# A four-layer attention and expert kernel: the first phase in another order, and layer 1's expert rows spread by token and choice

## The chip, the cores and the metric

The kernel runs on one core of a Trainium2 chip. The metric is the device time in microseconds of one execution. A core has TensorE (PE, its matrix engine, with PEld as its weight loads), VectorE (DVE), ScalarE (ACT), GpSimd (POOL) and SyncE (SP, which here only issues DMAs), each with its own instruction stream; they meet at semaphores.

## The reference

The input is x of 16 sequences x 128 tokens x 256 features, with a context of the same shape. Four layers each add an attention and a feed-forward part to x:

```
x = x + xattn0(layernorm(x), ctx)          # 16 heads, alibi bias and masks
x = x + ffn0(layernorm(x))                 # shared network + 8 experts on some rows
x = x + xattn1(layernorm(x), ctx)          # per token, among its 16 heads; no weights
x = x + moe1(layernorm(x))                 # 8 experts, 2 per token, hidden 512
x = x + xattn2(layernorm(x), ctx)
x = x + lora_int4(layernorm(x))
x = x + xattn3(layernorm(x), ctx)          # two attentions, three norms
x = x + moe3(layernorm(x))                 # 8 experts, 2 per token, hidden 1024
```

In moe1 a softmax over the router's 8 logits picks two experts for a token; the softmax of the two probabilities weighs their outputs: `out = sum_k weight_k * (silu(x @ gate_e) * (x @ up_e)) @ down_e`.

## The kernel before

The 2048 tokens are 16 tiles of 128, in four groups of four tiles. x stays on chip. The program has five stages.

**First phase** (31 to about 476 us). One group after another goes through layer 0 (keys and values of its context `kv`, query, attention in 8 units of two passes, output product `xo`, norm, shared network `up`/`down`, router logits `lg`). Layer 1's attention of the group before it runs beside that, on VectorE alone: it is cut into small *pieces* (`layer1_pieces`, L1761), and `some(n)` puts the next n pieces between VectorE's operations for layer 0, `until(x)` all of them up to mark x. The constants `L1_FRONT, L1_STEP = 10, 4` say how many pieces stand ahead of the first unit and behind each unit's row maxima (L1598). When the layer-1 rows of the previous group are normalised (`out_rows`), TensorE turns them (`xT3`), takes the router's logits (`lg1`), VectorE ranks the experts and finds each row's slot (`lists`, L1997), and POOL scatters the rows to the table `expert_rows_in` in DRAM with 8 indirect DMAs (`scatter`, L2484). TensorE's order in a group is: kv, xT0, q, attention, xo, xT3, lg1, xT1, shared network (with the rank product `rk` in it), lg. PSUM banks are given out by a planner in the order of the products, `k1` for group 0 and `k1f` for groups 1 to 3, which are one loop.

**Last rows** (to about 588). Layer 0's router and routed experts for the first rows, and beside them layer 1's pieces of group 3, then its list, the plan of which expert's weights each of the 39 tiles of expert rows takes (`plan_tiles`), and the last scatter.

**Experts of layer 1** (620 to 866). 39 tiles of 128 slots, in pairs (u = 0, 1). SP loads a tile's rows (L597), its expert's up and gate weights (L588, 1024 KB) and down weights (L592, 512 KB), and stores the 128 x 256 result to `expert_rows_out` (L623). ACT copies the result from PSUM (L1349).

**Phase 3** (870 to about 1278). Layers 2 and 3 by groups. For each group POOL gathers two rows of `expert_rows_out` for each token with 8 indirect DMAs (`gather`, L2493), and DVE adds them to x with their weights (`combine`, L2127 and `combine_second`, L2197, 8 `scalar_tensor_tensor` of 256 columns). At group 0 this stands before anything else; at the others it stands within the group before. Layer 3's list and scatter go to a second table, whose rows are 260 wide: 256 features, token, first expert and the weights.

**Experts of layer 3** (1278 to 1715). As those of layer 1, with more weights; here VectorE works out each slot's weight and token from the 4 extra columns (`keep_info` L2098, `slot_weights` L2080), ACT scales by the weight (L1353), and POOL adds the rows to the output with one accumulating indirect DMA per tile (L2634). SP loads the rows of a tile (L599) only when keep_info has copied the last ones' columns.

## Time and profile before

| | us |
|---|---|
| median of 3 runs | 1716.42 (1716.3 to 1718.08) |
| profiled execution | 1716.88 |
| its span | 1715.1 |
| PE busy | 1327.7 (77%) |
| PEld busy | 1078.8 (63%) |
| DVE busy | 832.6 (49%) |
| ACT busy | 433.3 (25%) |
| POOL busy | 287.6 (17%) |

The span is from the first to the last instruction of the profile; busy times are sums over the span, and the share of a stage can be far from that of the whole. The profile also names, for idle time of an engine, what ended it, and TensorE's granted clock of a stretch (PEclk, 1.00 is 2.4 GHz).

### The profile page before, as it was taken

The page shows a single profiled execution, that of the slowest core. Times are in us where ns is not written, and L with a number is a line of the kernel's source. Part 1 is how long each engine was busy: PE and PEld are TensorE (multiplying, and loading weights), DVE is VectorE, ACT ScalarE, POOL GpSimd, SP SyncE. Part 2 cuts the span into 40 slices and gives each one's busy share as a digit, 9 for nine tenths or more (in the row PEclk, how much of TensorE's full clock was granted, in tenths as well). Part 3 has the DMA queues.
Part 4 walks back from the last instruction along what each step waited for, and adds up shares of the span by engine and source line. Part 5 has one row for each costly group of instructions (what it writes and reads, how often), then busy time and mean ns, then how long its engine had stood idle before and what let it go on. Part 6 is the DMA issues. An engine that isn't in the chain of part 4 may idle for free. (4 is left out here: it accounts for less than half of the span.)

```text
span 1715.1 us, 26091 instructions
## 1 busy us (share of the span) xinstructions
PE 1327.7 (77%) x8177; PEld 1078.8 (63%) x8189; DVE 832.6 (49%) x2298; ACT 433.3 (25%) x1098; POOL 287.6 (17%) x306
## 2 busy tenths in 40 slices
PE   5877587685636248998988786877439999999997
PEld 3554444453423147888875565655329999999996
DVE  2258868778778731221233848485632222222222
ACT  2635245244112001111132232322101111111111
POOL 2010030020100020000023435351421111111111
PEclk9786686588777579999988898888759999999999
DMA  9992010010192258888820011100047888888884
GB/s 343 346 289 61 1 62 0 0 61 0 39 310 95 98 203 290 289 296 297 293 67 25 17 33 38 37 26 13 25 180 278 318 315 314 313 317 313 313 315 165
DMA packets 116307, 291.38 MB, mean 170 GB/s; under 512 B 8192, under 2 KB 90528, under 8 KB 101024
## 3 DMA queue, kind: packets, MB, share of 16 engines
q1 hardware_dynamic: 106032, 273.00, 45.5%
q0 software_dynamic: 10224, 17.77, 4.1%
q8 instruction: 24, 0.39, 0.1%
q14 instruction: 27, 0.22, 0.0%
HBM read 218.84 MB, written 71.90 MB: 170 GB/s over the span
## 5 line engine op out<-in xcount | busy, mean ns | idle before, releaser
L725 PE MATMUL bank<-norm_cols,work 128*128 128x128 f32 x3744 | 461.8, 277 | 20.8 <-DMA work<-in_moe 19.6
L725 PEld LDWEIGHTS bank<-norm_cols,work 128*128 128x128 f32 x3744 | 449.0, 193 | 38.8 <-issue 21.5
L1536 DVE TENSOR_TENSOR extra<-bank,span 128x256 f32<-128x256 f32 x234 | 99.2, 425 | 465.1 <-ACT span L1343 465.1
L725 PE MATMUL bank<-work,extra 128*128 128x256 f32 x936 | 240.0, 380 | 0.0
L1343 ACT ACTIVATE span<-bank 128x256 f32<-128x256 f32 x234 | 89.9, 384 | 541.9 <-PE bank L725 523.4
L725 PEld LDWEIGHTS bank<-work,extra 128*128 128x128 f32 x936 | 160.4, 191 | 12.5
L2634 POOL DMA_INDIRECT out_x<-att_rows,slot_token x39 | 60.7, 1556 | 378.0 <-ACT att_rows L1353 313.6
L2455 POOL TENSOR_TENSOR rstd<-var_eps,neg_half 128x4 f32<-128x4 f32 x17 | 17.3, 1018 | 501.6 <-DVE var_eps L1548 501.6
L725 PE MATMUL bank<-weights,norm_cols 128*128 128x512 f32 (+1 forms) x192 | 89.2, 614 | 12.2 <-ACT norm_cols L1374 5.5
L725 PE MATMUL bank<-work 128*128 128x256 f32 (+4 forms) x260 | 70.7, 418 | 28.0 <-ACT work L1374 12.7
L1280 ACT ACTIVATE work<-bank,row_max 128x128 f32<-128x128 f32 x256 | 69.8, 392 | 41.2 <-DVE row_max L1598 41.1
L824 PE MATMUL bank<-ident,work 128*128 128x128 f32 x256 | 53.5, 368 | 31.8 <-DVE att_rows L1536 24.7
L725 PEld LDWEIGHTS bank<-work 128*128 128x128 f32 (+1 forms) x260 | 45.6, 217 | 48.0 <-issue 20.0
L1598 DVE TENSOR_REDUCE row_max<-bank 128x4 f32<-128x512 f32 x64 | 41.1, 684 | 63.6 <-PE bank L725 63.6
L725 PE MATMUL bank<-norm_cols,weights 128*128 128x256 f32 (+1 forms) x160 | 59.2, 526 | 14.6 <-ACT norm_cols L1374 11.4
L824 PEld LDWEIGHTS bank<-ident,work 128*128 128x128 f32 x256 | 39.7, 187 | 48.7 <-DVE att_rows L1536 27.0
L725 PEld LDWEIGHTS bank<-weights,norm_cols 128*128 128x128 f32 x192 | 40.9, 226 | 46.3 <-issue 28.6
L966 PE MATMUL bank<-ident,att_cols 128*128 128x128 f32 x156 | 30.4, 277 | 46.3 <-DMA att_cols<-expert_rows_in 46.3
L2462 POOL TENSOR_TENSOR rstd<-var_eps,neg_half 128x2 f32<-128x2 f32 x48 | 35.5, 739 | 176.4 <-DVE var_eps L1548 175.9
L725 PEld LDWEIGHTS bank<-norm_cols,weights 128*128 128x128 f32 x160 | 36.2, 237 | 31.6 <-ACT norm_cols L1374 16.5
L966 PEld LDWEIGHTS bank<-ident,att_cols 128*128 128x128 f32 x156 | 21.9, 142 | 54.0 <-DMA att_cols<-expert_rows_in 46.5
L732 PE MATMUL bank<-ident,norm_rows_layer 128*128 128x128 f32 x32 | 7.9, 428 | 54.3 <-DVE norm_rows_layer L1554 54.3
(330 smaller groups left out, 1965.6 us busy)
## 6 DMA issues: line engine op xcount, KB each, us to landing
work<-in_moe SPq DMA_DIRECT2D x78, 1024.0 KB, 7.5
work<-in_moe SPq DMA_DIRECT2D x39, 2048.0 KB, 7.8
work<-in_moe SPq DMA_DIRECT2D x39, 512.0 KB, 6.1
expert_rows_in<-zero SPq DMA_DIRECT2D x3, 5590.0 KB, 47.1
expert_rows_in<-zero SPq DMA_DIRECT2D x3, 5504.0 KB, 36.0
expert_rows_out<-zero SPq DMA_DIRECT2D x3, 5504.0 KB, 33.7
att_cols<-expert_rows_in SPq DMA_DIRECT2D x39, 130.0 KB, 2.0
att_cols<-expert_rows_in SPq DMA_DIRECT2D x39, 128.0 KB, 3.3
```

Source lines behind the costliest of these rows:

```text
L725: return pe.matmul(o, l, r, start=a, stop=z)
L732: m = pe.transpose(ps[:, t * P:(t + 1) * P], rows[:, t, c * P:(c + 1) * P], ident[:, :])
L824: last = pe.transpose(ps[:, h * P:(h + 1) * P], SC[:, w, 4 * x + h, :], ident[:, :])
L966: last = pe.transpose(ps[:, c * P:(c + 1) * P], rows[:, u, c * P:(c + 1) * P], ident[:, :])
L1280: last = act.activation(SC[:, u, h, :], ps[:, (h % 4) * P:(h % 4 + 1) * P], ACT.Exp, bias=MX[:, 32 + 8 * u + h:33 + 8 * u + h])
L1343: act.activation(SG[:, b, :], ps[:, 0:256], ACT.Silu).then_inc(sem("silu_slots"), 1)
L1536: return dve.tensor_tensor(o, a, b, op)
L1598: last = dve.tensor_reduce(MX[:, at:at + 4], ps[:, :].rearrange("p (h k) -> p h k", h=4), AX, ALU.max, negate=True)
L2455: pool.tensor_tensor(RS[:, :], VE[:, :], neg_half[:, :], ALU.pow).then_inc(sem("rstd" + stream), 1)
L2462: pool.tensor_tensor(RS[:, part], VE[:, part], neg_half[:, part], ALU.pow).then_inc(sem(f"rstd_s{u}"), 1)
L2634: pool.indirect_dma_start(out=out_rows, out_offset=bass.IndirectOffsetOnAxis(ap=SLOTI[:, u:u + 1], axis=0), in_=YS[:, u, :], in_offset=Non ...
```

## The change

1. **Order of the first phase.** The keys and values of the next group are worked out behind `xo` of this one; the first norm of the next group stands within the shared network on VectorE. The turn, logits and ranks of layer 1's router for a group come one group later, within the attention (at units 1, 3 and 9), with VectorE's part of the list beside them. So phase 1 of group g treats the list of group g - 2; that of group 2 goes to the last rows. Fewer pieces stand in the attention, none between `xo` and the norm, and those left stand within and behind the shared network. The loop over groups is written out on all engines. SP loads the two context copies for layer 1 by separate semaphores.
2. **One table of rows.** Both layers use one `expert_rows_in` with rows of 260. Layer 1's rows now carry token, expert and weights as well. The second table, `expert_rows_out` and their zero stores go, as do the tables of slot index and weight per token.
3. **Layer 1's results spread.** As in layer 3, keep_info and slot_weights run for each tile, and ACT scales by the slot's weight. POOL writes the 128 rows of a tile with one indirect DMA (without accumulation) to `rows_by_choice`, at row token for the first choice and 2048 + token for the second; slots without a token go to spare rows. SP's store goes. In phase 1's end `plan_tiles` fills its table of expert and rows for both layers.
4. **Phase 3 loads plainly.** SP loads two blocks of 512 KB for each group, first and second choices, and VectorE adds each to x in one operation of 1024 columns. POOL's gathers go.

```diff
-L1_FRONT, L1_STEP, L1_SHIFT = 10, 4, 5
+L1_FRONT, L1_STEP = 7, 3
+LIST_STEPS = [0, 0, 0, 0, 3, 6, 1, 4]
+TURN_AT, LOGITS_AT, EXP_AT, PAIR_AT, RANKS_AT = 1, 3, 5, 9, 9
...
-        xs_dram = nc.dram_tensor("expert_rows_in", ((SPARE + 1) * SLOT, D), F32, kind="Internal").ap()
-        xs3_dram = nc.dram_tensor("expert_rows_in3", ((SPARE + 1) * SLOT, ROW), F32, kind="Internal").ap()
-        ys_dram = nc.dram_tensor("expert_rows_out", ((SPARE + 1) * SLOT, D), F32, kind="Internal").ap()
+        xs_dram = nc.dram_tensor("expert_rows_in", ((SPARE + 1) * SLOT, ROW), F32, kind="Internal").ap()
+        y1_dram = nc.dram_tensor("rows_by_choice", (2 * (NTOK + P), D), F32, kind="Internal").ap()
...
-                    if layer == 3:
-                        sp.wait_ge(sem(f"info_kept{u}"), count)
-                        sp.sem_inc(sem("sp_passed"), 1)
+                    sp.wait_ge(sem(f"info_kept{u}"), count + (0 if layer == 1 else LOOPS + 1 - u))
...
-                    sp.dma_start(ys_dram[ds(r * SLOT, SLOT), :], YS[:, u, :]).then_inc(sem(f"y_stored{u}"), 16)
...
+            def choice_rows(g):
+                if g == 0:
+                    for u in range(2):
+                        sp.wait_ge(sem(f"rows_spread{u}"), 16 * (LOOPS + (2 - u)))
+                else:
+                    sp.wait_ge(sem("combined"), g)
+                for k in range(2):
+                    at = k * NTOK + g * T * P
+                    sp.dma_start(YA[:, k, :].rearrange("p (t n) -> p t n", t=T), y1_dram[at:at + T * P, :].rearrange("(t p) n -> p t n", t=T)).then_inc(sem("choices_loaded"), 16)
...
+                    if a == "xT3":
+                        layer1_turned(plan, turn, listed)
+                    elif a == "lg1":
+                        layer1_logits(plan, turn)
+                    elif a == "rk":
+                        list_ranks(plan, turn, listed)
...
                 rows1(plan, turn, "xo", W0["o"], aT)
-                if prev is not None:
-                    layer1_logits(plan, turn, prev)
+                if g < GROUPS - 1:
+                    keys_values(plan, g + 1)
...
             def routed_start():
+                layer1_turned(jr0, 0, GROUPS - 2)
+                layer1_logits(jr0, 0)
...
+                        act.wait_ge(sem(f"slots_weighted{u}"), i + (1 - u + (0 if layer == 1 else LOOPS + 1 - u)))
                         if layer == 1:
-                            act.wait_ge(sem(f"y_stored{u}"), 16 * (i - u + PRIMED))
-                            act.activation(YS[:, u, :], ps[:, 0:D], ACT.Copy).then_inc(bank_empty[b], 1)
+                            act.wait_ge(sem(f"rows_spread{u}"), 16 * (i + (1 - u)))
...
+                        act.activation(YS[:, u, :], ps[:, 0:D], ACT.Copy, scale=SLOTW[:, u:u + 1]).then_inc(bank_empty[b], 1)
...
                 for n in range(UNITS):
                     maxima(n)
                     some(L1_STEP)
-                    if n == L1_SHIFT:
-                        until("shifted")
+                    weights(LIST_STEPS[n])
                     if n >= 6 and n % 2 == 0:
                         norm_out((n - 6) // 2)
...
-                some(L1_STEP)
+                places(3)
                 norm_out(T - 1)
-                until("end")
+                until("shifted")
+                places(8)
...
-                if prev is not None:
-                    logits_out(plan, turn)
-                    lists(plan, turn, prev, prev, True)
+                some(4)
...
+                    some(2)
+                    if i == 1 and g < GROUPS - 1:
+                        first_stats(g + 1)
+                    if i == 2 and g < GROUPS - 1:
+                        first_rows(g + 1)
                     if i > 1:
                         add_y(i - 2)
+                        some(2)
                 add_y(T - 2)
+                some(1)
                 add_y(T - 1)
...
+                until("end")
...
-                some(4)
+                weights(14)
+                some(1)
...
                     routed_pairs(g)
+                    if g == 0:
+                        places(11)
...
                     if s[0] == "xsT":
-                        if layer == 3:
-                            if kind != "start" or s[1] == 0:
-                                slot_weights(s[1], i - s[1])
-                            keep_info(s[1], 2 * i + (2 - s[1]))
+                        if kind != "start" or s[1] == 0:
+                            slot_weights(layer, s[1], i - s[1])
+                        keep_info(layer, s[1], i + (1 - s[1]))
                         rows_out(plan, turn, s[1])
...
+                if layer == 1:
+                    dve.wait_ge(sem(f"rows_spread{u}"), 16 * (n + 1))
+                else:
+                    dve.wait_ge(sem(f"rows_added{u}"), n + PRIMED)
...
+            def combine(g, k):
+
+                x = X[:, ds(g * T * D, T * D)]
+                dve.wait_ge(sem("choices_loaded"), 32 * (g + 1))
+                settle()
+                i = tt(x, x, YA[:, k, :], ALU.add)
...
+            def phase1(g, sent):
+                prev = g - 1
+                if g > 0:
+                    power(2 * prev + 1, "_l1")
+                power(2 * g + 2)
+                if sent == 0:
+                    pool.wait_ge(sem("lists_zeroed"), 16 * zrows.shape[0])
+                if sent is not None:
+                    scatter(sent, NA)
+                if g < GROUPS - 1:
+                    power(2 * g + 3)
+                    x_bias(g + 1)
+                if g > 0:
+                    power(2 * prev + 2, "_l1")
...
+            def spread(u):
+                pool.indirect_dma_start(out=y1_dram, out_offset=bass.IndirectOffsetOnAxis(ap=SLOTI[:, u:u + 1], axis=0),
+                                        in_=YS[:, u, :], in_offset=None).then_inc(sem(f"rows_spread{u}"), 16)
```

## Rows read from the trace of the kernel before

**Rows 1.** Windows by stretch: us, busy of each engine, PEclk, DMA share, GB/s
```profile
134.00:248.00 114.00, 83.22 (x440) 54.37 (x442) 88.33 (x182) 43.55 (x117) 12.16 (x11) 0.69 0.10 30
248.00:362.00 114.00, 81.43 (x437) 52.81 (x439) 86.37 (x181) 43.49 (x116) 9.11 (x9) 0.70 0.05 17
...
619.00:870.00 251.00, 229.40 (x1672) 209.23 (x1672) 52.91 (x126) 45.81 (x121) 0.57 (x2) 0.99 0.83 279
```

**Rows 2.** DVE timeline, first phase: start, us, line, operation, idle before and its releaser
```profile
39.61 1.29 DVE L1598 TENSOR_REDUCE row_max<-bank 128x4 f32<-128x512 f32 x2 [16.06 <-PE bank L725]
...
130.21 1.29 DVE L1598 TENSOR_REDUCE row_max<-bank 128x4 f32<-128x512 f32 x2 [0.27 <-PE bank L725]
...
251.10 1.29 DVE L1598 TENSOR_REDUCE row_max<-bank 128x4 f32<-128x512 f32 x2 [5.50 <-PE bank L725]
...
290.55 1.29 DVE L1598 TENSOR_REDUCE row_max<-bank 128x4 f32<-128x512 f32 x2 [5.20 <-PE bank L725]
...
308.30 0.42 DVE L1536 TENSOR_TENSOR att_rows<-bank,row_rec 128x256 f32<-128x256 f32 x1
...
313.81 0.41 DVE L1536 TENSOR_TENSOR products_dve<-extra,ctx_rows_by_dim 128x256 f32<-128x256 f32 x1
...
320.02 1.23 DVE L1536 TENSOR_TENSOR extra<-extra,row_rec 128x1024 f32<-128x1024 f32 x1
...
333.83 0.19 DVE L1867 COPY small<-bank 128x32 f32<-128x32 f32 x1 [0.26 <-PE bank L725]
...
344.49 1.28 DVE L1536 TENSOR_TENSOR work<-bank,work 128x256 f32<-128x256 f32 x3
...
476.58 0.29 DVE L1661 TENSOR_REDUCE row_max<-router_logits 128x16 f32<-128x128 f32 x1 [5.26 <-ACT router_logits L1306]
```

**Rows 3.** Timeline of PE, first phase
```profile
95.03 1.97 PE L732 MATMUL bank<-ident,norm_rows 128*128 128x128 f32 x8 [5.47 <-DVE norm_rows L1554]
...
113.13 1.07 PE L732 MATMUL bank<-ident,ctx_rows 128*128 128x128 f32 x8
...
122.11 1.04 PE L732 MATMUL bank<-ident,norm_rows 128*128 128x128 f32 x8
...
311.53 6.71 PE L725 MATMUL bank<-weights,att_cols 128*128 128x256 f32 x16 [0.78 <-ACT att_cols L1254]
327.38 1.97 PE L732 MATMUL bank<-ident,norm_rows_layer 128*128 128x128 f32 x8 [9.14 <-DVE norm_rows_layer L1554]
```

**Rows 4.** Experts of layer 1: timelines of SP, DVE, ACT, and the waits
```profile
712.57 0.35 SPq L597 DMA_DIRECT2D att_cols<-expert_rows_in  x1
714.20 0.33 SPq L588 DMA_DIRECT2D work<-in_moe  x1
...
710.88 0.42 DVE L1536 TENSOR_TENSOR extra<-bank,span 128x256 f32<-128x256 f32 x1 [2.96 <-ACT span L1343]
...
714.28 0.38 ACT L1349 ACTIVATE att_rows<-bank 128x256 f32<-128x256 f32 x1 [0.56 <-PE bank L725]
...
PE bank L725 <- DMA work<-in_moe: 19.6, 22, 1.6
```

**Rows 5.** Experts of layer 3: timelines of DVE and SP
```profile
1491.39 0.42 DVE L1536 TENSOR_TENSOR extra<-bank,span 128x256 f32<-128x256 f32 x1 [2.23 <-ACT span L1343]
...
1494.15 0.33 SPq L599 DMA_DIRECT2D att_cols<-expert_rows_in  x1
```

**Rows 6.** DMA issues by line: median us to landing is last
```profile
expert_rows_out<-att_rows SPq DMA_DIRECT2D x39, 128.0 KB, 5.0
...
out_x<-att_rows,slot_token POOLq DMA_INDIRECT x39, 9.4
```

**Rows 7.** Start of phase 3: timelines of POOL, DVE, PE
```profile
870.25 1.19 POOL L2500 DMA_INDIRECT extra<-expert_rows_out,slot_index_gather  x1 [0.91 <-POOL slot_index_gather L2495]
...
882.47 1.67 DVE L2133 SCALAR_TENSOR_TENSOR x_stream<-extra,combine_weight_group,x_stream 128x256 f32<-128x256 f32 x4 [9.79 <-DMA extra<-expert_rows_out,slot_index_gather]
...
890.20 0.66 PE L1007 MATMUL bank<-ident,norm_rows 128*128 128x128 f32 x4 [3.19 <-DVE norm_rows L2214]
```

More of the change, by code:

```diff
@@ L853, in phase1 @@
                     if s == "up":
-                        if i == 2 and prev is not None:
-                            list_ranks(plan, turn, prev)
                         ps, b = fill(plan, turn, ("up", i))
@@ L2001, in lists, with plan_tiles @@
                 settle()
-            def plan_tiles(rows):
+            def plan_tiles():
                 J = MOE_TILES
@@ L2078, in rows_out, with slot_weights @@
                 dve.tensor_copy(xsT[:, u, :, :], ps[:, 0:D].rearrange("p (c n) -> p c n", c=KC)).then_inc(bank_empty[b], 1)
-            def slot_weights(u, n):
+            def slot_weights(layer, u, n):
                 token, chosen, more, second, expert, rows = (INFO[:, u, i:i + 1] for i in range(6))
-                first, held, far = (SLOTT[:, u, i:i + 1] for i in range(3))
+                first, held, far, later = (SLOTT[:, u, i:i + 1] for i in range(4))
+                spare = DUMP[:, u:u + 1] if layer == 1 else DUMP[:, 2:3]
+                stt = dve.scalar_tensor_tensor
```

446 lines of the change are left out of this document (218 added, 228 removed).

## The prediction, made before the changed kernel was run

> **What bounds the kernel now.** I read the table of stretches first [rows 1]. The mixture-of-experts stage of layer 1 is a stage of TensorE and the weight stream: TensorE is busy 229.40 of 251 us with the DMA queues at 0.83. The first phase is not: in 134 to 248 and 248 to 362 us, VectorE is busy 88.33 and 86.37 of 114, TensorE 83.22 and 81.43 at a granted clock of 0.69 and 0.70. Neither is full, so the order in which they hand over to each other decides, and much of TensorE's work there runs at the lower of its two clock levels (1.2 of 2.4 GHz). Next I read the timelines. A period of a group goes from one first row maximum (L1598) to the next, 251.10 - 130.21 = 120.9 us, ahead of a middle group [rows 2]; I cut the group from 251.10 into A, the attention of layer 0, until the last normalised output (308.7, 57.6 us); B, until the first gate product of the shared network (344.49, 35.8 us, where the row shows work<-bank,work); then the shared network (7.2) and the tail to the next first maximum (20.3), both from the same timeline. In A VectorE idles 5.20 us at 290.55. In B the old order serves value pieces, then xo, then lists (333.83 to 344.49, 10.7 us), while TensorE waits 9.14 us at 327.38 and works at half clock: xo takes 6.71 us at 311.53 [rows 2, 3]. Last come the experts of layer 1, where TensorE's waits for weights are 19.6 us in 22 places, and the start of phase 3 [rows 4, 7].
>
> **Phase 1, part by part.** The DVE work per group hardly changes; it is regrouped. Costs: eight score or value pieces of a tile are 6.2 us (313.81 to 320.02); the list is 10.7 us less its 3.52 wait for ranks, so 7.1 [rows 2].
> A: 8 maxima (9.6 us, 1.2 each as at 251.10), 30 pieces instead of more than 40 (about 25.3), output norms 2.6, list weights 4.1: 42 us of DVE work. Old A carried 57.6 with about 8 us of idling. New A: 42 + 8 = 50 in groups 2 and 3, 48 in group 1, which has no list but is then paced by TensorE and ScalarE. Bounds: 45 (group 0's attention, without pieces, takes about 44 us from its first maximum at 39.6) and 57 (as now).
> B: no value pieces, no list. DVE work about 10.8 us, so the chain is TensorE's: attention turn, xo, keys and values of the next group (9.0 us at full clock, 113.13 to 122.11), turn, first up product: 17.6 at full clock. At half clock about 32, as xo has doubled (6.71, against 3.7 for the same product at full clock). I take 22, since TensorE comes from a busy attention; was 35.8 [rows 3].
> Shared network: DVE now puts 10 pieces and the first norm of the next group among its products: 7.2 becomes 17.5 (14 in group 3, which has no next). Bounds 14 to 18.5.
> Tail: 21 pieces stay for the end, about 20.4 us (17 value pieces, division, addition, norm and its rows), and the 7.75 us of front pieces of the next group: 28.2 us, was 20.3. TensorE has only about 12 us of work in it, so it idles some 16 us and begins the attention cold.
> Period: 48 + 22 + 17.5 + 28.2 = 115.7 for group 1 (was 120.9, -5.2) and 117.7 for group 2 (was 121, -3.3). Group 0 to 1: keys and values fill the 5.47 us wait before 95.03 and the first maximum no longer waits for them (122 instead of 130.21): -8. Its context load must land before about 89; it is issued after 56 us behind the zero stores, and the queue has been done by about 80. If it were late, the 8 is gone. Group 3: 50 + 22 + 14 + 20.4 = 106.4 against 104.6 from its first maximum to 476.58: +1.8, which already counts that the 5.26 us wait for the router's logits goes [rows 2, 3].
> The list of group 2 moves into the stage of last rows, where DVE is the busy engine: three more operations than today because facts are kept in the row; 7.1 + 0.8 less what falls into gaps of about 1 us there: +5.5. The last list grows by 0.5. POOL's scatter of eight DMAs, 10.3 us, now stands behind the second norm's power and before the next; its queue is idle there, so nothing is late by it. Zero stores go from three tables to one: they lie beside phase 1 and nothing waits for them, 0. Sum of phase 1: -8 -5.2 -3.3 +1.8 +5.5 +0.5 = **-8.7**, with all the uncertainty of the clock: with A 46 and B 19 in three groups it is 19 less, with A 53 and B 25 it is 19 more. The outer ends, A 57 and B 32, would be near 50 more, but suppose half clock all through, and rows 1 show 0.69 even with the waits of now.
> TensorE's granted clock is what rows 1 and 3 show: 0.69 and 0.70 where it waits for VectorE. Of this the Trainium skill (TensorE: Matmul & The Clock Gate, section What's actually happening) says that the throttled state is the default and activity releases it. That agrees, and speaks against this change: the waits are gathered in one idle stretch before each attention rather than spread. By the rule the cold start of A costs a little of the 50; it is the half-clock rival below.
>
> **Experts of layer 1.** A tile takes 251 / 39 = 6.4 us. SP issued the rows load at 712.57 and the next up weights at 714.20, in program order [rows 4]. Now the rows load waits for keep_info, which stands behind slot_weights on DVE. Layer 3 shows that very order: product at 1491.39, rows load 1494.15, so 2.76 from product to rows load [rows 5]. In layer 1 the product that stands there is at 710.88: the rows load would come at 713.64 instead of 712.57, and the up load, 1.3 behind it as in layer 3's timeline, at 714.95 instead of 714.20: 0.75 us later (0.85 with the one more operation). Queued behind the rows load: the up load, the down load, and through them TensorE. If the stage is bound by latency, half of it is paid per tile: +0.4 x 39 = +15. If it is bound by bandwidth (279 GB/s, DMA share 0.83, waits that never pass 1.6 us), a later issue only shortens the queue: 0. The rows lie nearer the second, since several waits per pair remain even with early issues; I take **+4**. DVE's extra two microseconds per tile lie in its waits: it is busy 52.91 of 251 [rows 1]. The spread on POOL replaces SP's store byte for byte, and POOL is idle. Layer 3's experts lose one small operation, 0; plan_tiles' five more operations of 0.48 lie in a wait of 10 us for the first rows, 0.
> The spread adds a wait: slot_weights may not overwrite the indices before the spread of the same buffer has landed. In old time slot_weights would begin at 711.3, behind the product at 710.88, and the eviction of that buffer ends at 714.66, 3.4 us later; the next slot_weights on the same buffer is due two tiles (12.6 us) after the first, 9.2 after the eviction; POOL needs 1 us to start, as at 870.25. So about 8 us are free from issue to landing. The direct store of the same 128 KB landed in 5.0 us, the accumulating indirect one of layer 3 in 9.4 [rows 4, 6, 7]. Bounds: 0, and 9.4 - 8.2 = 1.2 us in two tiles, 0.6 per tile, +24. Without accumulation I take it nearer 5: 0.
> The Trainium skill (DMA: Bandwidth & Descriptors, section Anatomy of one DMA, SWDGE path) gives 2.0 us plus bytes over 436 GB/s, an estimate of 2.3 us for this transfer, so no wait at all. The 9.4 of the trace is far from it; by the page the term stays 0.
>
> **Phase 3.** Before: eight gathers from 870.25, DVE combines from 882.47, TensorE waits 3.19 us until 890.20 and 0.94 for the second half [rows 7]. After: the last spread lands at about 871, two 512 KB loads about 877, two additions of 1.23, norm rows at about 885, before TensorE runs out at 887. The wait goes: **-4.1** (at least 3.2; the larger end if the rows are there in time, which needs the loads to land before 879). Next late is TensorE itself. The combines of groups 1 to 3 fall by 2 us of DVE each, but stand beside waits for ScalarE and TensorE: 0 (down to -2 each). 24 gathers leave POOL, which waits anyway: 0.
>
> **Sum.** -8.7 + 4 - 4.1 = -8.8 from the profiled execution's 1716.88 us (span 1715.1 and 1.8 around it) is 1708.1; that execution stood 0.5 above the median of the runs, 1716.42, so I say **1707.5**.
>
> **The rivals.**
> 1. TensorE stays near full clock through A and B (A 46, B 19 in three groups): period about 111, 19 us less: **1688**. For it: B has no DVE in its chain now. Against: 16 idle us before each attention.
> 2. Slower: the spread's landing holds DVE in the experts of layer 1. From 8 us on it decides; at 9.4, +24: **1732**. For it: the only indirect store with a measured landing takes 9.4. Against: that one also reads its target, and stores of the scatter seem to be through within 5 to 8.
> 3. The delayed rows and up loads are paid in full, +15 instead of +4: **1719**. For it: 22 waits for weights already.
> 4. Half clock: A 53 and B 25 while the tail grows; phase 1 comes out at about +10 instead of -8.7: **1726**. For it: the idle stretches, gathered in one place before A. Against: a whole attention keeps TensorE busy by itself, and group 0's takes only 44.
> 5. The change moves nothing: what VectorE is freed of is filled by waits of the same length, phase 1 near 0, phase 3 start hidden: **1716**.
>
> **How the numbers follow.** The forecast has 0.38, rival 1 0.16, rival 2 0.13, rival 3 0.14, rival 4 0.11, rival 5 0.08. A measurement of this kernel tells about 0.2% (3.4 us) from no change. Faster: 0.38 and 0.16, with a third of rival 5 and a little of rival 3: 0.58. Same: 0.16. Slower: rivals 2 and 4 and part of 3: 0.26. The range is 1684 to 1733: it takes in rivals 1, 3, 4 and most of 2, and leaves out about 0.2. The forecast's own range is 1700 to 1714.
>
> **What would show it.** In the profile after: period from first maximum to first maximum of 116 to 118 us; A near 50; the gap between xo and xT1 filled with keys and values; TensorE idle about 16 us ahead of each attention; first maximum of group 1 at 122. In the experts: tile time 6.4 to 6.5, waits for weights not above 25 us, and no wait of slot_weights for the spread. At phase 3: TensorE not idle after its product ending at 887 in old time. Wrong would be: a period under 112 or over 120, a tile of 6.8 or more, or DVE waiting on a DMA of rows_by_choice.

## The result, and the profile after

The changed kernel takes 1743.99 us (median of 4 runs, 1738.17 to 1750.75), the kernel before 1717.25 beside it (4 runs, 1716.3 to 1722.08): ratio 1.0178, 95% interval 1.015 to 1.0207, so 1.8% slower. A second comparison on another occasion gave 1744.1 and 1.0174 (1.0148 to 1.02). The profiled execution took 1738.17 us with a span of 1736.4, 21.3 more than the 1715.1 of before. It is the fastest of the four executions, 5.8 us under their median, so the table below accounts for 21.3 of the 26.7 us between the medians. Forecast were 1707.5 and a range of 1684 to 1733.

I cut both traces at the same events. A, B and rest are the parts of a group as in the prediction (rest is shared network and tail).

| stage | before | after | difference | forecast |
|---|---|---|---|---|
| up to the first maximum of group 0 | 39.6 | 40.0 | +0.4 | 0 |
| group 0 (A, B, rest) | 90.6 (44.2, 18.3, 28.1) | 90.5 (44.2, 27.0, 19.3) | -0.1 | -8 |
| group 1 | 120.9 (57.0, 35.1, 28.8) | 117.8 (50.3, 21.6, 45.9) | -3.1 | -5.2 |
| group 2 | 120.9 (57.6, 35.8, 27.5) | 129.9 (62.4, 21.5, 46.0) | +9.0 | -3.3 |
| group 3 | 104.6 (56.5, 35.6, 12.5) | 117.5 (62.3, 21.5, 33.7) | +12.9 | +1.8 |
| last rows and last list | 144.6 | 150.9 | +6.3 | +6.0 |
| experts of layer 1 | 244.0 | 254.9 | +10.9 | +4 |
| start of phase 3, to its first norm turn | 25.1 | 21.8 | -3.3 | -4.1 |
| phase 3 | 388.1 | 373.6 | -14.5 | 0 |
| experts of layer 3 | 436.8 | 439.5 | +2.7 | 0 |

The rest of the document is about four of these rows: groups 2 and 3, group 0, the experts of layer 1, and phase 3, which gave back 14.5 us that the forecast did not have.

The same stretches of the profile after, by windows (us, busy us of each engine, granted clock, DMA share, GB/s), beside [rows 1]:

```profile
134.00:248.00 114.00, 82.70 (x432) 52.87 (x432) 83.39 (x155) 42.87 (x110) 7.33 (x5) 0.72 0.05 14
248.00:362.00 114.00, 83.90 (x438) 54.51 (x440) 80.10 (x157) 45.05 (x121) 13.65 (x11) 0.69 0.04 15
```

In the second window VectorE is busy 80.10 us instead of 86.37 while TensorE has 438 instructions in place of 437: VectorE has less to do, and TensorE gets no more done.

VectorE's timeline after. The first, second, second-last and last lines are marks of the table. The four between them are maxima of the attention of group 2, with the idle time before them in brackets, and the third-last line belongs to the third of its four output norms; A ends at 310.68, behind the fourth:

```profile
130.43 1.29 DVE L1639 TENSOR_REDUCE row_max<-bank 128x4 f32<-128x512 f32 x2 [1.55 <-PE bank L727]
...
248.26 1.28 DVE L1639 TENSOR_REDUCE row_max<-bank 128x4 f32<-128x512 f32 x2
...
260.69 1.29 DVE L1639 TENSOR_REDUCE row_max<-bank 128x4 f32<-128x512 f32 x2 [1.66 <-PE bank L727]
...
269.58 1.29 DVE L1639 TENSOR_REDUCE row_max<-bank 128x4 f32<-128x512 f32 x2 [5.29 <-PE bank L727]
...
277.53 1.29 DVE L1639 TENSOR_REDUCE row_max<-bank 128x4 f32<-128x512 f32 x2 [4.20 <-PE bank L727]
...
293.19 1.29 DVE L1639 TENSOR_REDUCE row_max<-bank 128x4 f32<-128x512 f32 x2 [5.20 <-PE bank L727]
...
307.65 0.26 DVE L1646 RECIPROCAL row_rec<-bank 128x16 f32<-128x16 f32 x1 [2.63 <-PE bank L831]
...
378.19 1.28 DVE L1639 TENSOR_REDUCE row_max<-bank 128x4 f32<-128x512 f32 x2
...
495.72 0.28 DVE L1707 TENSOR_REDUCE row_max<-router_logits 128x16 f32<-128x128 f32 x1
```

In [rows 2] one such maximum inside A had a wait of 5.20. Here there are three of 4.2 to 5.3 us. The windows of exactly A of group 2, before and after (VectorE is the third engine):

```profile
251.10:308.70 57.60, 39.07 (x276) 24.33 (x277) 48.66 (x72) 30.28 (x86) 0.79 (x1) 0.69 0.00 0
248.26:310.68 62.42, 41.56 (x298) 26.90 (x298) 41.50 (x77) 29.28 (x88) 0.00 (x0) 0.63 0.03 9
```

VectorE's idle time in A is 57.60 - 48.66 = 8.9 us before and 62.42 - 41.50 = 20.9 after. In group 1 after, which has no list, the same window has 37.17 busy and 13.1 idle. What TensorE waited for in the same attention stands in its own timeline:

```profile
251.89 1.01 PE L727 MATMUL bank<-work,ident_bf 128*128 128x512 bf16 x2 [9.11 <-ACT work L1311]
...
256.60 1.97 PE L838 MATMUL bank<-ident,work 128*128 128x128 f32 x8 [1.69 <-ACT k_cols L1270]
...
264.72 1.95 PE L727 MATMUL bank<-w_router,k_cols 128*128 128x8 f32 x16 [2.46 <-ACT work L1317]
...
272.94 1.12 PE L838 MATMUL bank<-ident,work 128*128 128x128 f32 x4 [2.35 <-DVE small L1915]
...
288.04 1.11 PE L838 MATMUL bank<-ident,work 128*128 128x128 f32 x4 [3.18 <-DVE att_rows L1568]
```

Three of these five waits belong to the list, 6.5 us together. 1.69 is for the bank of the router's turned rows (xT3), until ScalarE has copied them to k_cols. 2.46 is ahead of the router logits (lg1), for the probabilities (ACT work L1317) that were last turned in that bank. 2.35 is the turn of the next probabilities, held until VectorE has copied the logits out of the bank (small L1915). LIST_RING gives xT3 and lg1 banks of the probabilities' ring, so each list step puts a handshake with a second engine into the attention's own double buffering. That the waits are there, and on whom, is read from the trace; no run has the list inside the attention with banks of its own, so what the shared ring costs, apart from the steps themselves, is not shown.

### The profile page after: what moved, and what is told of

It reads as the page before. It is cut to its first block and busy times, and to the rows that moved or that the text cites. A ratio compares the mean times of both kernels' runs of the same rounds, so it can differ in the third digit from the quotient of the medians.

```text
span 1736.4 us, 25826 instructions
## 1 busy us (share of the span) xinstructions
PE 1319.2 (76%) x8189; PEld 1071.0 (62%) x8189; DVE 865.5 (50%) x2595; ACT 436.0 (25%) x1098; POOL 299.4 (17%) x315
## 3 DMA queue, kind: packets, MB, share of 16 engines
q1 hardware_dynamic: 71520, 238.34, 39.6%
## 5 line engine op out<-in xcount | busy, mean ns | idle before, releaser
L727 PE MATMUL bank<-norm_cols,work 128*128 128x128 f32 x3744 | 463.3, 278 | 28.5 <-DMA work<-in_moe 27.3
L1568 DVE TENSOR_TENSOR extra<-bank,span 128x256 f32<-128x256 f32 x234 | 99.0, 424 | 437.1 <-ACT span L1374 431.7
L727 PE MATMUL bank<-work 128*128 128x256 f32 (+4 forms) x260 | 69.9, 414 | 27.3 <-ACT work L1404 12.3
L727 PE MATMUL bank<-weights,norm_cols 128*128 128x512 f32 (+1 forms) x192 | 75.5, 536 | 8.6 <-ACT norm_cols L1404 5.5
L2659 POOL DMA_INDIRECT rows_by_choice<-att_rows,slot_token x41 | 39.3, 959 | 225.2 <-ACT att_rows L1383 224.6
L727 PE MATMUL bank<-norm_cols,weights 128*128 128x256 f32 (+1 forms) x160 | 60.3, 532 | 14.7 <-ACT norm_cols L1404 11.7
L727 PEld LDWEIGHTS bank<-weights,norm_cols 128*128 128x128 f32 x192 | 35.2, 193 | 36.7 <-issue 25.0
```

The lines of the kernel that those rows point to most:

```text
L727: return pe.matmul(o, l, r, start=a, stop=z)
L1568: return dve.tensor_tensor(o, a, b, op)
L2659: pool.indirect_dma_start(out=y1_dram, out_offset=bass.IndirectOffsetOnAxis(ap=SLOTI[:, u:u + 1], axis=0), in_=YS[:, u, :], in_offset=None ...
```

## Experiments

Each kernel starts from the changed one, except where it says before. Ratios are to the kernel before, in the same comparison, whose median for the kernel before lay between 1707.15 and 1717.25 us; 95% intervals in brackets; stage times come from each kernel's own trace, cut as in the table.

**e1: the list out of the attention.** Its turn, logits, exponentials and ranks go behind xo, with banks from the ordinary ring. ScalarE's and VectorE's parts of it move along, and POOL works out the next group's first norm and bias ahead of the scatter and not behind it; the cut below shows a part of the edit. All else stays.

```diff
-            for a, i in att_steps(listed is not None):
+            for a, i in att_steps(False):
...
                 rows1(plan, turn, "xo", W0["o"], aT)
+                if listed is not None:
+                    layer1_turned(plan, turn, listed)
                 if g < GROUPS - 1:
                     keys_values(plan, g + 1)
+                if listed is not None:
+                    layer1_logits(plan, turn)
...
                 norm_out(T - 1)
                 until("shifted")
-                places(8)
```

> The changed kernel, but the layer-1 list of groups 0 and 1 is taken out of the attention: its turn stands behind xo, its logits behind the keys and values, its ranks and VectorE's part around the first products of the shared network. Theory list (the list inside the attention holds TensorE and its banks): the attention stretch A of groups 2 and 3 falls from 62 to 64 us to about 50 us, as in group 1, the stretch B after it grows by about 3 us; together -18 us, so about 1726 us. Theory clock (the attention is long only because TensorE starts it cold, after the idle stretch): A stays at 58 to 62, the time at 1738 to 1750.

Measured: 1726.77, ratio 1.0109 (1.0049 to 1.0168). A is 50.3 in groups 2 and 3, from 62.4 and 62.3; those groups take 126.0 and 107.6, and the router's maximum comes at 477.69 instead of 495.72: 18.0 us earlier, 1.1 behind the kernel before. Groups 2 and 3 give 13.8 of the 18.0: A falls by 24.1, but B of group 2 grows by 5.4 and the rest, which now has the list, by 2.8 and 2.6. The other 4.2 lie ahead of group 2, where the edit changes nothing of the list. TensorE's timeline of e1 at the start of the same attention, and the window of its A:

```profile
247.65 1.01 PE L731 MATMUL bank<-work,ident_bf 128*128 128x512 bf16 x2 [16.52 <-ACT work L1317]
```

```profile
244.02:294.30 50.28, 35.53 (x268) 22.42 (x268) 37.16 (x55) 28.05 (x84) 0.00 (x0) 0.70 0.03 11
```

TensorE idled 16.52 us ahead of it, more than after's 9.11, ran its first transposes at the lower clock level (1.01 us, against 0.61 for the same two at the higher), and A was still 50.3. So the idle stretch before the attention doesn't cost the 12 us; the list inside does. Of the 12.1, TensorE's busy time has 6.0 (41.56 to 35.53) and its other time 6.1, about the 6.5 of the three waits. Of the 6.0, about 2.4 are the list's own products (an estimate from their rows, 1.95 of it the logits); the rest goes with the granted clock inside A, which is 0.63 with the list and 0.70 without. Whether that lower clock is a consequence of the waits isn't separated. In the total 12 us of the gain show (1.0178 to 1.0109, with intervals that overlap); 5.3 went into the experts of layer 1, 260.2 in this trace.

**e2: the second group's context load ahead of the zero stores.**

```diff
+            b, n = job(jk, ("cT", 1), 0)
+            sp.wait_ge(bank_full[b], n + 1)
+            sp.dma_start(CG[:, :, :], ctx_in[T:2 * T, :, :]...).then_inc(sem("ctx_loaded"), 16)
             sp.wait_ge(sem("zero_set"), 1)
             for i in range(zrows.shape[0]):
...
-                next_ctx1(1)
```

> The changed kernel, but SP issues the context load of group 1 ahead of the three zero stores. Theory transfer (the 8 us that group 0 was to save were lost because this context lands at 94 us, behind the zero stores): TensorE's wait of 4.3 us goes, its clock stays up, the first row maximum of group 1 comes at 122 us instead of 130.4: -8, about 1736 us. Rival (VectorE's first pieces set that maximum anyway): it stays at 129 to 130, 0 us, 1744.

The profile after has the cause in SP's timeline (start, us) and TensorE's:

```profile
25.64 38.88 SPq L560 DMA_DIRECT2D expert_rows_in<-zero  x2
64.57 32.02 SPq L567 DMA_DIRECT2D ctx_rows<-in_ctx  x2
```

```profile
94.22 1.97 PE L734 MATMUL bank<-ident,ctx_rows 128*128 128x128 f32 x8 [4.34 <-DMA ctx_rows<-in_ctx]
...
96.92 3.75 PE L727 MATMUL bank<-ctx_cols,weights 128*128 128x512 f32 x4 [0.73 <-issue]
```

The row of 64.57 holds two loads. The first is the one that group 0 waits for: its issue alone took 20.65 us, and it landed 29.6 behind its start, at 94.2.

This is what e2 makes of it, in SP's timeline, then TensorE's, then VectorE's:

```profile
20.26 5.12 SPq L560 DMA_DIRECT2D ctx_rows<-in_ctx  x1
25.42 40.40 SPq L563 DMA_DIRECT2D expert_rows_in<-zero  x3
```

```profile
89.41 1.04 PE L736 MATMUL bank<-ident,ctx_rows 128*128 128x128 f32 x8
```

```profile
122.01 1.29 DVE L1641 TENSOR_REDUCE row_max<-bank 128x4 f32<-128x512 f32 x2 [1.70 <-PE bank L729]
```

Group 0 takes 83.1 us, B 18.7 of them, and the first maximum of group 1 stands at 122.01; the prediction said 122. The router's maximum comes 9.0 us earlier than after. In the total, 1736.41 and 1.0175 (1.0136 to 1.0215), this can't be told from after: the experts of layer 1 were 258.2 in this trace, and the interval is 14 us wide.

**e3 and e8: spare matmuls ahead of each attention of groups 1 to 3**, 40 (two TensorE instructions each) and 12, against the theory that the clock at the start of A makes it long.

```diff
                     elif a == "s":
+                        if g > 0 and i == 2:
+                            spare, _ = fill(plan, turn, ("acc", "oT", 0))
+                            for _ in range(40):
+                                mm(spare[:, 0:256], W0["o"][:, 0, 0:P], W0["o"][:, 0, :])
```

> The changed kernel with 40 products of 128 x 256 without use on TensorE in groups 1 to 3, in its idle stretch before the third score product; results unchanged. Theory clock: the granted clock at the start of the attention is 1.0 instead of 0.5, A falls to about 52 in groups 2 and 3 and 45 in group 1: -25 us, about 1719. Theory list: banks and waits of the list stay, A falls to 58 to 60 in groups 2 and 3: -8 us, about 1736.

> As the kernel with 40 products without use in groups 1 to 3, but with 12, which end inside TensorE's idle stretch. Theory clock: the attention begins warm and A falls from 62 to 52 to 56 in groups 2 and 3, 50 to 46 in group 1: -15 to -20 us against the changed kernel. Rival (the clock falls again within the attention, whatever it starts with, because waits interrupt it): A within 2 us of 62, 62 and 50, 0 us.

e3: 1763.46, 1.0348 (1.0299 to 1.0397). It was badly sized: the 80 instructions took 19.04 us in TensorE's timeline and ran into the attention, so A of 63.5, 69.1, 69.1 tells of the filler.

```profile
256.15 19.04 PE L727 MATMUL bank<-weights 128*128 128x256 f32 x80
```

e8: 1738.72, 1.0130 (1.0086 to 1.0175); A 51.5, 64.5, 64.8. The first 24 us around the start of group 2's attention had a granted clock of 0.68 instead of 0.59, the next 24 had 0.53 instead of 0.70. The attention was no shorter, it was 2.1 and 2.5 longer. This shows that the idle stretch ahead of it isn't what makes it long, which e1 showed too. It doesn't show what a full clock through the whole of A would give, since the clock fell again (0.60 over A of group 2).

**e4: the list's VectorE work one piece earlier**, LIST_STEPS [0,0,0,0,3,6,1,4] to [0,0,0,3,0,6,1,4].

> The changed kernel, but VectorE copies the list's logits out of their bank one unit earlier (three list operations stand behind the fourth row maxima instead of the fifth). Theory bank (the probabilities' turn waits for the bank of the logits): the waits of 2.35 us in groups 2 and 3 go, with what follows -2 to -4 us in each: about 1738. Rival (VectorE then waits for the logits in that place and the next maxima come later): 0 or up to +3 us, 1744 to 1747.

1730.85, 1.0146 (1.0103 to 1.0189); A 59.4 and 61.8. It frees the logits' bank sooner and gets 3.0 and 0.5 of the 12 us. The wait of 2.35 is gone in both groups. In group 3 TensorE's busy time in A rises instead, from 41.46 to 43.80 us at a granted clock of 0.61 in place of 0.64: there one wait less brought almost nothing. The period of group 2 falls by 5.8, since its B is 18.7 here; why B takes 18.7 in some traces and 21.5 in others was not looked into.

**e5: SP's order in the experts of layer 1**, up load before rows load; and at the end the last two slot_weights behind the last products. **e12** has only the second edit.

```diff
+                        filled(plan, turn, ("up", 0, h - 1))
+                        load_up(0, 2 * i + 2)
                         filled(plan, turn, ("xsT", 1))
                         if more:
                             info_kept(1, i + 1)
                             load_rows(1, 2 * i + 3)
-                        filled(plan, turn, ("up", 0, h - 1))
-                        load_up(0, 2 * i + 2)
```

> The changed kernel, but in the experts of layer 1 SP issues the up weights of a tile ahead of the rows that wait for VectorE's copy, and the last two slot_weights stand behind the last products instead of ahead of them. Theory order (the 11 us more of this stage come from up weights that are issued 0.8 us later, and 3 to 4 of them from the wait for the spread's landing at its end): the stage falls from 252 to 260 us to 244 to 247, the time by about 10 us against the changed kernel (ratio to before about 1.012). Rival queue (the spread's indirect writes disturb the weight stream, whatever SP's order): only the end's 3 us go, the stage stays at 250 to 256.

> The changed kernel, with only the last two slot_weights of layer 1's experts moved behind the last products, SP's order as changed. VectorE's wait of 1.0 and 2.7 us for the spread's landing leaves TensorE's path: -2 to -4 us, the stage about 3 us shorter than in the changed kernel; the rest of what the order edit gained is then SP's order. Rival: 0.

In the profile after, a tile of this stage in SP's, VectorE's and TensorE's timelines, and the stage's waits (us, times, longest), beside [rows 4]:

```profile
715.94 0.34 SPq L603 DMA_DIRECT2D att_cols<-expert_rows_in  x1
717.22 0.34 SPq L595 DMA_DIRECT2D work<-in_moe  x1
```

```profile
713.06 0.42 DVE L1568 TENSOR_TENSOR extra<-bank,span 128x256 f32<-128x256 f32 x1 [2.77 <-ACT span L1374]
```

```profile
713.52 1.95 PE L727 MATMUL bank<-norm_cols,work 128*128 128x128 f32 x16
```

```profile
PE bank L727 <- DMA work<-in_moe: 27.3, 30, 1.9
```

and e5: SP, waits, and 150 us of the stage:

```profile
703.38 0.34 SPq L595 DMA_DIRECT2D work<-in_moe  x1
704.87 0.34 SPq L603 DMA_DIRECT2D att_cols<-expert_rows_in  x1
```

```profile
PE bank L741 <- DMA work<-in_moe: 2.6, 5, 1.2
```

```profile
700.00:850.00 150.00, 149.38 (x1100) 137.77 (x1099) 63.31 (x316) 32.27 (x78) 24.93 (x26) 1.00 0.91 320
```

e5 takes 1721.12 (10 runs), 1.0042 (1.0016 to 1.0068); the stage falls from 254.9 to 228.5 us, 15.5 below the kernel before, where 244 to 247 was expected. Its waits for weights go from 27.3 us to 2.6, and the queues deliver 320 GB/s where after has 281 and before 294 over the same 150 us. In after the up load comes 1.8 us behind the end of the up products (717.22 - 715.47), in e5 0.9 (703.38 - 702.49). e12: 1744.53, 1.0149 (1.0105 to 1.0193), stage 253.7: of the 26.4 us the second edit has at most 1.2, where about 3 was expected.

**e10: the same order in the kernel before.**

> The kernel before, with one edit: in the experts of layer 1 SP issues the up weights of a tile ahead of its rows. Theory issue (that stage is set by when SP issues the up weights, not by the bandwidth of the queues): 0.7 us earlier per tile, the stage falls from 244 to 225 to 235 us, ratio about 0.99 to 0.995. Theory bandwidth (as the forecast had it: 279 to 297 GB/s is what the queues give): 244, ratio 1.000.

1715.42, 0.9994 (0.9976 to 1.0012); stage 241.6, from 244.0, so the 225 to 235 of the issue theory did not come. In before the rows load was already out when the up products ended, so the swap brought the up load no nearer: 0.9 us behind them at the least in both, 0.92 and 0.98 in the median. So the order alone doesn't make e5's 228.5; that leaves the store, which is no longer SP's in e5, for the rest. Two kernels ask what of the store costs, its bytes or its issue.

**e13 and e14: e10 with the store cut.** e13 stores 16 of each tile's 128 rows (the other 112 are left out), e14 stores none (the results of layer 1's experts are left out of everything behind them).

```diff
-sp.dma_start(ys_dram[ds(r * SLOT, SLOT), :], YS[:, u, :])...
+sp.dma_start(ys_dram[ds(r * SLOT, 16), :], YS[0:16, u, :])...   (e13)
+sp.sem_inc(sem(f"y_stored{u}"), 16)                              (e14)
```

> The kernel before with the up weights issued first, and SP's store of each tile of layer 1's experts cut from 128 rows to 16: its issue and its waits stay, 7/8 of its bytes go. Left out: the other 112 rows of each tile's result. Theory bytes (the store's 128 KB in the queue of the weights cost the stage its 6 to 13 us): the stage falls from 242 to 230 to 236. Theory issue (SP's time for one more DMA and its waits): it stays at 240 to 244.

> As the kernel with the small store, but SP issues no store at all; it keeps the waits. Left out: the results of layer 1's experts. Theory bytes: the stage as with the small store, 230 to 236. Theory issue: 228 to 236 here, against 240 to 244 with the small store.

e13: 1707.26, 0.9951 (0.9933 to 0.9969), stage 238.2. e14: 1690.86, 0.9860 (0.9837 to 0.9883), stage 226.1. Storing an eighth of the bytes gains 3.4 us, which lies between the two expectations and within what stages of one code differ by here; no store at all gains 12.1 more. ScalarE waits for no store's landing in either, so the 12.1 go with SP's issue and its address load, the two things that e14 drops beside the last 16 rows. SP's timelines, e13 first:

```profile
703.41 0.35 SPq L588 DMA_DIRECT2D work<-in_moe  x1
704.76 0.33 SPq L597 DMA_DIRECT2D att_cols<-expert_rows_in  x1
706.09 0.33 SPq L592 DMA_DIRECT2D work<-in_moe  x1
707.50 0.35 SPq L623 DMA_DIRECT2D expert_rows_out<-att_rows  x1
708.85 0.35 SPq L588 DMA_DIRECT2D work<-in_moe  x1
```

```profile
704.33 0.34 SPq L588 DMA_DIRECT2D work<-in_moe  x1
705.69 0.34 SPq L597 DMA_DIRECT2D att_cols<-expert_rows_in  x1
707.07 0.35 SPq L592 DMA_DIRECT2D work<-in_moe  x1
710.05 0.34 SPq L588 DMA_DIRECT2D work<-in_moe  x1
```

Consecutive DMAs of SP stand 1.33 to 1.41 us apart though each shows 0.34 busy. Four per tile make 5.44 us (708.85 - 703.41), which is nearly all the time a tile of TensorE's needs in these stages (5.7) and leaves SP 0.3 for its waits. With three there is a gap of 2.98 before the next up load, and that load leaves when its buffer comes free. So SP's issue time, far more than the store's bytes, is what bounds layer 1's experts in the kernel before, next to TensorE itself, and moving the store to POOL is worth some 13 us there once the rows load is out of the way (241.6 to 228.5; e9 and e11 had 235.6 and 235.0, so it may be as little as 6; why these two are 7 above e5 was not looked into).

**e6 and e7: the clock at the start of phase 3.** e6 is the kernel before with 14 spare matmuls ahead of the first turn of phase 3; e7 the changed kernel with ten additions on VectorE ahead of its first combine, so that TensorE waits.

```diff
+                    if g == 0:
+                        spare, _ = fill(plan, turn, ("xT4", 0))
+                        for _ in range(14):
+                            mm(spare[:, 0:256], W3["v4"][:, 0, 0:P], W3["v4"][:, 0, :])
                     for u in streams:                                      (e6, before)
...
                 if before is None:
+                    for _ in range(10):
+                        d(tt(wide[:, 0, :], wide[:, 1, :], wide[:, 1, :], ALU.add))
+                        settle()
                     combine(g, 0)                                          (e7, after)
```

> The kernel before, with 14 products of 128 x 256 without use on TensorE in its wait of 3.2 us at the start of phase 3. Theory clock (the first group of phase 3 took 12 us less after the change because TensorE no longer paused, and so kept its full clock): the granted clock of the 30 us behind it is 1.0 instead of 0.57 to 0.80, phase 3 is 6 to 12 us shorter though the products themselves last up to 3 us longer than the wait; net -4 to -10 us against before. Rival (it was the gathers' or combines' work that went): 0 to +3 us.

> The changed kernel, with 10 additions of 128 x 312 without use (about 0.5 us each) on VectorE ahead of the combine of phase 3's first group. Theory clock: TensorE pauses about 3.5 us before the turn of the query rows, its clock halves as before the change, and the time grows by 3.5 + 5 to 8 us, about +10 against the changed kernel. Rival: by the pause alone, +3.5.

The two windows behind the first turn (the granted clock is the third number from the end), in before, after, e6 and e7:

```profile
890.00:914.00 24.00, 20.23 (x74) 15.38 (x74) 9.83 (x26) 6.54 (x16) 6.44 (x6) 0.66 0.00 0
914.00:938.00 24.00, 18.99 (x68) 12.35 (x67) 5.59 (x20) 6.46 (x17) 9.38 (x11) 0.84 0.15 44
```

```profile
923.00:947.00 24.00, 17.01 (x88) 12.69 (x88) 11.85 (x36) 8.21 (x19) 5.31 (x7) 1.00 0.00 1
947.00:971.00 24.00, 20.16 (x106) 14.60 (x105) 8.67 (x28) 10.18 (x29) 2.79 (x4) 1.00 0.00 1
```

```profile
891.00:915.00 24.00, 17.55 (x87) 13.46 (x85) 11.95 (x36) 7.53 (x18) 5.08 (x6) 0.93 0.00 1
915.00:939.00 24.00, 21.47 (x100) 15.36 (x101) 5.33 (x18) 8.51 (x24) 9.37 (x11) 0.93 0.15 44
```

```profile
923.00:947.00 24.00, 20.41 (x74) 15.50 (x74) 9.70 (x25) 6.55 (x16) 6.44 (x6) 0.67 0.04 15
947.00:971.00 24.00, 20.23 (x76) 13.46 (x77) 5.49 (x19) 7.27 (x18) 1.41 (x2) 0.83 0.00 0
```

e6: 1710.94, 0.9981 (0.9957 to 1.0006), not told apart from before in the total; the start takes 2.8 us more for the filler, phase 3 behind it 380.5, 7.6 less. e7: 1747.3, 1.0206 (1.0161 to 1.0251), not told apart from after's 1.0178 in the total; TensorE pauses 1.96 and 0.94 us, phase 3 takes 383.9, 10.3 more. The traces of the other kernels say how far that stage moves by itself: 386.4 to 388.1 in the three with before's phase 3 and the pause, 373.1 to 380.6, in the mean about 376, in the eleven with after's and no pause. With the pause TensorE gets 74 instructions done in 24 us, without it 87 or 88, whichever kernel it is. e14, which has before's gathers and combines but no pause (granted clock 0.98 in the 24 us behind its turn), shows 377.4.

**e9 and e11: the three repairs together**, e1, e2 and e5; e11 has SP's new order in layer 3's experts too.

> The changed kernel with the three edits together: the list out of the attention, group 1's context ahead of the zero stores, and in the experts of layer 1 the up weights issued ahead of the rows, the last slot_weights behind the products. If they add: -18 -9 -16 to -26 against the changed kernel, so about 0.98 to 0.985 of the kernel before. Rival (what one gains early another waits for later): 0.99 or more.

> As the kernel with the three edits, and SP's new order in the experts of layer 3 as well. TensorE is busy there for 417 to 425 of 437 us, so there is little to win: 0 to -5 us against the kernel with the three edits; rival (the rows come later and TensorE waits for them): +2 to +5.

e9: 1699.94, 0.9913 (0.9881 to 0.9945). e11: 1697.74, 0.9899 (0.9871 to 0.9928). Both beat the kernel before and the changed one, by less than the 0.98 to 0.985 that the single gains add up to. In e9 the groups take 84.1, 117.4, 127.7, 107.7 us, the router's maximum stands at 476.75 (before: 476.58), the experts of layer 1 take 235.6, and phase 3 376.6. So even mended, phase 1 gains nothing over before: the gain is in the experts of layer 1 (-8.4), the start of phase 3 (-3.3) and phase 3 behind it (-11.5), less the 6.4 that the last rows and lists take more. e11's extra edit can't be told from e9 (intervals overlap; layer 3's experts 437.1).

**e15: the changed kernel again**, to have a second comparison of it.

> The changed kernel again. By the traces so far: periods of 118, 130 and 117.5 us, attention stretches of 50, 62 and 62, the experts of layer 1 in 252 to 260 us, phase 3 in 373 to 381; ratio to before 1.015 to 1.02. Rival: another stage than these carries part of the loss in other executions.

1744.1, 1.0174 (1.0148 to 1.02), as told above; group 0 88.0, A of groups 2 and 3 62.4 and 62.3, experts 259.1, phase 3 376.4.

## Why the prediction was wrong

**A = 42 + 8 in groups 2 and 3: the step that failed most.** The prediction summed VectorE's work in A (42 us) and carried its idle time over from the old A (8 us). The work came out at 42. The idle came out at 20.9. Of the 12.9 too little, about 5 have nothing to do with the list: in group 1, which has none, VectorE is busy 37.2 and idle 13.1, so the 8 was already wrong there, and A was 50.3 only because there was less work. The other 7.8 come with the list, since the change doesn't only put the list's VectorE operations there (4.3 us of them) but also its TensorE and ScalarE steps, in the banks through which the attention hands its probabilities over. The sum counted the engine that was busiest and not the handshakes. Cost: 12.4 and 12.3 against the forecast. e1 takes 24.1 out of the two attentions and 13.8 out of the two groups, with the list's work paid elsewhere. The half-clock rival gave a time nearer the result, 1726, by the idle stretch ahead of A, which e1 and e8 exclude as the reason. The clock inside A is another matter: it was 0.63 with the list and 0.70 without, about 3.6 of the 12.1 us by the estimate beside e1, and whether the waits brought it down is open.

**Group 0, -8.** The prediction said that the load must land before 89, that it is issued behind the zero stores, and that "the queue has been done by about 80". It landed near 94, since that load was issued at 64.57, and keys and values ran at half clock behind the wait (B 27.0). "If it were late, the 8 is gone" is what happened, all of it (-0.1); e2 makes the condition true and gets 122.01. The mechanism was right, the reading of when the queue would be empty was wrong: SP's timeline shows the issue of the zero stores itself blocking for 38.88 us, which the landing times don't.

**Experts of layer 1, +4.** The delay was right: the up load forecast 0.85 later, measured 0.84 (4.16 us behind VectorE's product, 3.32 in [rows 4]). The choice between latency and bandwidth was wrong. I took 279 GB/s and a DMA share of 0.83 for a bound, but the same queues run at 320 in e5. Over nine traces with this order the stage averages 256.2 (252.3 to 260.2), 12.3 above the two of before (244.0, 243.7): near the +15 of rival 3. That nearness is luck. The 12.3 are a balance: with the order mended e5, e9 and e11 show 228.5 to 235.6, so the delay costs 21 to 28, and the rest of the change in this stage, in the main the store that left SP, gives 8 to 15 of it back. What the prediction missed behind it is that SP was itself the tight resource, which turns "the spread replaces SP's store byte for byte, 0" from a nothing into one of the two real gains of the change; phase 3 has the other.

**Spread on POOL, no wait: right.** The view of the spread's line in after (who waited, us, times; then the landings):

```profile
  DVE slot_work L2129: 3.7, 2
...
DMA to landing us min/median/max: 3.0/5.7/8.1
```

Only the last two slot_weights wait, 3.7 us together; the budget of 8.2 was enough, and the 9.4 of [rows 6], an accumulating write, was no measure for this one. The Trainium skill (DMA: Bandwidth & Descriptors, section Anatomy of one DMA, SWDGE path) would give the estimate of 2.3 us named in the prediction; the trace has 3.0 at the least and 5.7 in the median, so the page is too low here, though it decides nothing.

**Start of phase 3, -4.1: right**, -3.3 measured, and the norm turn follows without a wait, as TensorE's timeline of after shows beside [rows 7]:

```profile
921.52 1.88 PE L727 MATMUL bank<-ctx_cols,products_dve 128*1 128x512 f32 x4
923.33 1.09 PE L1022 MATMUL bank<-ident,norm_rows 128*128 128x128 f32 x8
```

**Phase 3 behind it, 0: wrong by 14.5**, 11.7 of it up to the first turn of its second group (87.6 us before, 75.9 after). Over all the traces counted beside e6 and e7 the difference is about 11, so this pair shows it large. I costed the 3.19 us wait of [rows 7] at its own length. It also dropped the granted clock to 0.66 for the next 24 us. e7 puts a pause back and loses 10.3, e6 takes the pause out of before and gains 7.6. With e14, where before's phase 3 runs without the pause and is nearly as short as after's, the pause and the clock behind it explain nearly all of it; for the lighter combines and gathers 1 or 2 us may be left, which the traces don't resolve. The forecast missed the result by 36.5 us; without this gain, which it didn't have, it would have missed by more. The Trainium skill (TensorE: Matmul & The Clock Gate, section What's actually happening) puts the penalty of the ramp, the time at the lower clock before TensorE is released, at under 1% of a typical kernel's time. One pause cost 7.6 us in e6 and 10.3 in e7, 0.4 and 0.6% of 1715, so that agrees in size, and it was still as large as the largest term that I had added up, the 8 of group 0.

**Right as sized:** B 21.5 (22), shared network and tail 46.0 (45.7), last rows and last list +6.3 (+6.0). B won 14 us per group by having VectorE out of its chain. The tail took 18 back and A should have had the remaining gain.

**Chances.** The measured 1743.99 lies above every rival. The one that held best, 3, had 0.14. None had the list's steps in A, 25 us over two groups against the forecast. I had listed a clock mechanism for a long A and no mechanism of waits and buffers.

## What to carry to other kernels

When steps move into a pipelined loop, cost them on every engine that they touch and follow the buffers that they share: work that fits an engine's idle time can still add a handshake to the loop's double buffering (12 us per attention here, for 4.3 us of VectorE work in it). Before taking a DMA stage to be bandwidth-bound, count the issuing engine's DMAs per tile times the spacing between its issues; if that is close to the tile's time, the order of the issues and their number matter, and the bytes little. A wait of 3 us that ends a full-clock stretch may be worth two to three and a half times its length in what follows (7.6 for 3.19 in e6, 10.3 for 2.9 in e7).

## What the runs showed of the hardware

- SP's DMAs in this loop, each with its wait and its address from a register, stand 1.24 us apart at the least and 1.34 to 1.44 in the median, while the profile shows 0.34 us each: four in 5.44 us fill the issuing engine and would count as 25% busy.
- Two issues of zero stores (5.6 MB each) blocked SP's queue for 38.88 us. A 512 KB load behind them, of a kind that lands in 3.7 us in the median, began its issue at 64.57, was 20.65 us in it and landed 29.6 us after its start. Ahead of them it left at 20.26.
- An indirect 128 KB write from POOL takes 0.96 us to issue and 3.0 to 8.1 to land; the accumulating one 1.56, and 9.3 to land in the median.
- The bandwidth-bound look of the experts' weight stream (279 GB/s) wasn't one: the same weights in the same pieces ran at 320 with TensorE busy 149.4 of 150 us.
- TensorE's clock behind a short pause: 0.66 and 0.67 over 24 us with a pause before it (3.19 and 0.94 us, 1.96 and 0.94), 0.93 to 1.00 without. A granted 1.0 is 2.4 GHz; 0.66 is a stretch that lay for the larger part at 1.2.
